# A five-layer perceiver block: the last stage's weights rounded during the sign MLP and kept in device memory

## The reference, cut to what matters

```python
# sign MLP: weights are +1 or -1 by a boolean (k0, k1, k2)
h = s0 * _conn_dense(k0, concatenate([x, -x])); h = relu(h) * 2
h = s1 * _conn_dense(k1, h);                    h = relu(h) * 2
h = s2 * _conn_dense(k2, h)                     # 1024 -> 2048 -> 2048 -> 512

def _act_fake_quant(x, clip_factor):
    scale = sigmoid(clip_factor) * max(abs(x)) / 127
    return clip(round(x / scale), -128, 127) * scale
def _weight_fake_quant(w):
    scale = max(abs(w), axis=1, keepdims=True) / 127
    return clip(round(w / scale), -128, 127) * scale
xq   = _act_fake_quant(x, clip_x)
gate = einsum('bsh,ih->bsi', xq, _weight_fake_quant(w_gate))     # w_gate, w_up: 1408 x 512
up   = einsum('bsh,ih->bsi', xq, _weight_fake_quant(w_up))
h    = _act_fake_quant(silu(gate) * up, clip_down)
out  = einsum('bsi,hi->bsh', h, _weight_fake_quant(w_down))      # w_down: 512 x 1408
```

## Time and profile before

| what | value |
|---|---|
| time, median of 3 runs | 1179.59 us (1178.83 to 1183.53) |
| profiled execution, its own time | 1179.79 us |
| its span in the profile | 1178.0 us |
| mean granted clock of TensorE | 0.974 of full speed |
| sign MLP: end of its second half's layer 0 / of its output layer | 489.2 / 627.4 us |
| last stage: first instruction / end | 1060.7 / 1178.0 us |

### The profile page before, as it was taken

One profiled execution on the slowest core, in us unless ns is written; L12 is line 12 of the kernel. 1 busy time (PEld: TensorE's weight loads), 2 busy tenths in 40 slices (PEclk: granted clock), 3 DMA queues, 4 the chain that ended last, 5 costly groups with the idle time before them and its releaser, 6 DMA issues. The chain is left out here.

```text
span 1178.0 us, 17300 instructions
## 1 busy us (share of the span) xinstructions
PE 1080.0 (92%) x6279; PEld 679.8 (58%) x6300; DVE 597.3 (51%) x1020; ACT 388.1 (33%) x1038; POOL 214.9 (18%) x205
## 2 busy tenths in 40 slices
PE   7899999999899999999999999776898989985976
PEld 4456568887444444444445655374796968663542
DVE  2344356786733222421113544277658484758857
ACT  1222245666310001201001322243324232337863
POOL 0111101333322310070000111043141221200004
PEclk9899999999999999999999999978999999996999
DMA  9966802001011100300034788340000000008001
GB/s 337 386 231 228 299 1 73 1 1 37 27 36 42 38 0 1 103 13 0 0 143 143 265 304 296 149 163 1 2 0 1 0 0 0 0 0 294 1 1 71
DMA packets 55127, 108.60 MB, mean 92 GB/s; under 512 B 4144, under 2 KB 4528, under 8 KB 55088
## 3 DMA queue, kind: packets, MB, share of 16 engines
q1 hardware_dynamic: 55088, 108.09, 25.9%
HBM read 105.98 MB, written 2.10 MB: 92 GB/s over the span
## 5 line engine op out<-in xcount | busy, mean ns | idle before, releaser
L1769 ACT ACTIVATE f_act<-bank,f_sgn 128x512 f32<-128x512 f32 x64 | 44.0, 687 | 267.8 <-PE bank L1724 262.3
L1724 PE MATMUL bank<-f_a_hi,f_w 128*128 128x512 f16 x512 | 115.7, 379 | 0.0
L1724 PE MATMUL bank<-f_a_lo,f_w 128*128 128x512 f16 x512 | 115.7, 379 | 0.0
L1798 DVE CAST f_b_hi<-f_act 128x512 f32 x32 | 27.1, 848 | 164.3 <-ACT f_act L1769 164.3
L1724 PEld LDWEIGHTS bank<-f_a_lo,f_w 128*128 x512 | 50.1, 98 | 60.4
L1724 PEld LDWEIGHTS bank<-f_a_hi,f_w 128*128 x512 | 50.1, 98 | 60.2
L1574 DVE TENSOR_TENSOR s_e<-s_pair,s_tables 128x512 f32<-128x512 f32 x64 | 41.4, 687 | 42.0 <-POOL s_kT L1634 24.8
L397 PE MATMUL bank<-x_cT,x_qT 128*64 128x512 f32 x256 | 60.0, 613 | 0.0
L422 PE MATMUL bank<-x_cN,x_eT 128*64 128x512 f32 x256 | 56.9, 596 | 0.0
L698 POOL TENSOR_TENSOR x_mv<-x_mv,eps 128x2 f32<-128x2 f32 x9 | 1.7, 193 | 292.8 <-DVE x_mv L568 292.8
L1456 ACT ACTIVATE s_e<-bank,s_nmax 128x64 f32<-128x64 f32 x128 | 38.0, 336 | 50.8 <-DVE s_nmax L1520 50.8
(11 more groups left out here) (337 smaller groups left out, 2305.3 us busy)
## 6 DMA issues: line engine op xcount, KB each, us to landing
x_cT<-in_ctx_cols_dram SPq DMA_DIRECT2D x32, 1024.0 KB, 8.2
x_cN<-in_ctx_rows_dram SPq DMA_DIRECT2D x32, 1024.0 KB, 9.7
f_upper_bits<-in_f_w_dram SPq DMA_DIRECT2D x20, 256.0 KB, 2.7
s_wv_raw<-in_s_wv_dram SPq DMA_DIRECT2D x3, 1024.0 KB, 10.3
f_raw<-in_f_wd_dram SPq DMA_DIRECT2D x1, 2816.0 KB, 17.6
x_qw<-in_x_qw_dram SPq DMA_DIRECT2D x8, 256.0 KB, 4.8
x_kw<-in_x_kw_dram SPq DMA_DIRECT2D x8, 256.0 KB, 5.6
x_vw<-in_x_vw_dram SPq DMA_DIRECT2D x2, 1024.0 KB, 9.6
```

The lines of the kernel that those rows point to most:

```text
L1724: mm = pe.matmul(h_bank[s][:, :], weights(2 * i + s, k), part[:, k, cols], start=(n == 0 and k == 0), stop=(n == 1 and k == k_chunks - 1))
L1769: act.activation(act32[s][:, :], h_bank[s][:, :], ACT.Relu, scale=sgn[:, layer % 2:layer % 2 + 1]).then_inc(h_read, 1)
L1798: dve.tensor_copy(hi[:, 2 * i + s, :], act32[s][:, :]).then_inc(hhi_ok, 1)
```

## The change

The last stage no longer scales, rounds and transposes weights. A new class `Rounding` keeps, through the whole kernel, the row maxima, steps and inverses of the three matrices, and reserves device memory for the three rounded bf16 matrices in the layout of the matmul (`[P, KC, I]`, `[P, KC, I]`, `[P, IC, D]`). The host passes, beside the raw matrices, their transposes (`f1_wgT`, `f1_wuT`, `f1_wdT`). Working buffers lie over the sign MLP's first-layer weights, booleans and first-layer inputs.

In `sign_mlp`:
- SyncE, once the booleans of layer 2 are converted, loads the 26 row chunks of the raw matrices (22 of [128, 512] in four slots, 4 of [128, 1408] in one), stores the inverses of the three matrices and the steps of down to device memory, and waits for that. After `h_done >= 3 * HC` it loads, for each of 27 parts of the transposed matrices (8 + 8 of [128, 704], 11 of [128, 512]), the part, and at the start of a matrix the broadcast row of its inverses; it stores the rounded parts. Two buffers alternate for parts in and for parts out. It ends with a wait for all stores, ahead of the next stage's loads.
- VectorE takes the row maxima, 22 of them between the output tiles of the first half and 4 before layer 1 of the second, and then makes steps and inverses.
- GpSimd takes each part through a product with the inverse row, an addition and a subtraction of 1.5 * 2^23, the last one to bf16, each behind a wait for the one before; at its end it waits for all stores.

In `quantized_ffn` SyncE loads the clip scalars, gate, up, the row of down steps and down. ScalarE's first wait is for the clip scalars and the row of steps. Tokens are transposed through four banks instead of two, and the products of chunk 0 wait for their half of the tokens alone.

```diff
+class Rounding:
...
+        half = I // 2
+        self.matrices = []
+        for rows, cols, kept in ((io["f1_wg"], io["f1_wgT"], self.gate), (io["f1_wu"], io["f1_wuT"], self.up)):
+            parts = [{"width": half, "span": I, "at": slice(h * half, (h + 1) * half), "src": cols[k * P:(k + 1) * P, h * half:(h + 1) * half],
+                      "dst": kept[:, k, h * half:(h + 1) * half]} for k in range(KC) for h in range(2)]
...
         @block.sync
         def _(sp):
...
+            sp.wait_ge(w2_ok, W2_RAW)
+            for n, (m, c) in enumerate(rows):
+                slot = n % RAW if m < 2 else 0
+                if n >= RAW:
+                    sp.wait_ge(wmax_ok, n - RAW + 1 if m < 2 else n)
+                sp.dma_start(maxima_raw[m][slot], matrices[m]["rows"][c]).then_inc(row_in[slot], 16)
+            sp.wait_ge(wstep_ok, 4)
+            for m in range(3):
+                sp.dma_start(rounding.inverse_out[m], w_inv[m], allow_slow_non_contiguous=True).then_inc(inv_out, 16)
+            sp.dma_start(rounding.step_out, w_step[2], allow_slow_non_contiguous=True).then_inc(inv_out, 16)
+            sp.wait_ge(inv_out, 16 * 4)
+            sp.wait_ge(h_done, 3 * HC)
+            for n, (m, a) in enumerate(parts):
+                part = matrices[m]["parts"][a]
+                if a == 0:
+                    if n:
+                        sp.wait_ge(scaled_ok, n)
+                    sp.dma_start(inv_row[:, 0:part["span"]], rounding.inverse_row[m].partition_broadcast(P)).then_inc(inv_in, 16)
+                if n >= 2:
+                    sp.wait_ge(rounded_ok, 2 * (n - 1))
+                sp.dma_start(raw_part[n % 2][:, 0:part["width"]], part["src"]).then_inc(part_in[n % 2], 16)
+                if n:
+                    last = matrices[parts[n - 1][0]]["parts"][parts[n - 1][1]]
+                    sp.wait_ge(rounded_ok, 2 * n)
+                    sp.dma_start(last["dst"], rounded_out[(n - 1) % 2][:, 0:last["width"]]).then_inc(part_out[(n - 1) % 2], 16)
...
+            sp.wait_ge(part_out[0], 16 * ((len(parts) + 1) // 2))
+            sp.wait_ge(part_out[1], 16 * (len(parts) // 2))
...
         @block.vector
...
+                    if half == 1 and layer == 1:
+                        row_maxima(range(2 * HALF_ROWS, len(rows)))
+                        dve.wait_ge(wmax_ok, len(rows))
+                        dve.tensor_scalar(rounding.all_step, rounding.all_max, 1.0 / QMAX, None, ALU.mult).then_inc(wstep_ok, 1)
...
+                    if half == 0:
+                        row_maxima(range(2 * HALF_ROWS * t // (HT // P), 2 * HALF_ROWS * (t + 1) // (HT // P)))
...
         @block.gpsimd
...
+            for n, (m, a) in enumerate(parts):
...
+                pool.wait_ge(inv_in, 16 * (m + 1))
+                pool.wait_ge(part_in[n % 2], 16 * (n // 2 + 1))
+                pool.tensor_tensor(raw_part[n % 2][:, 0:width], raw_part[n % 2][:, 0:width], inv_row[:, part["at"]], ALU.mult).then_inc(scaled_ok, 1)
+                pool.wait_ge(scaled_ok, n + 1)
+                pool.tensor_scalar(raw_part[n % 2][:, 0:width], raw_part[n % 2][:, 0:width], ROUND, None, ALU.add).then_inc(rounded_ok, 1)
+                pool.wait_ge(rounded_ok, 2 * n + 1)
+                if n >= 2:
+                    pool.wait_ge(part_out[n % 2], 16 * (n // 2))
+                pool.tensor_scalar(rounded_out[n % 2][:, 0:width], raw_part[n % 2][:, 0:width], ROUND, None, ALU.subtract).then_inc(rounded_ok, 1)
...
+def quantized_ffn(core, tag, weights, clips, out):
...
         @block.sync
         def _(sp):
             sp.dma_start(clip_in[:, :], clips.partition_broadcast(P)).then_inc(small_in, 16)
-            for g, cs in enumerate(groups):
-                at = slice(cs[0], cs[-1] + 1)
-                for m in range(2):
-                    sp.dma_start(raw[m][:, at, :], views[m][:, at, :]).then_inc(raw_in[m][g], 16)
-            sp.dma_start(raw[2][:, :, :], views[2]).then_inc(down_in, 16)
+            sp.dma_start(gT[:, :, :], weights.gate).then_inc(gate_in, 16)
+            sp.dma_start(uT[:, :, :], weights.up).then_inc(up_in, 16)
+            sp.dma_start(d_row[:, :], weights.step_row.partition_broadcast(P)).then_inc(small_in, 16)
+            sp.dma_start(dT[:, :, :], weights.down).then_inc(down_in, 16)
...
         @block.scalar
-            act.wait_ge(small_in, 16)
+            act.wait_ge(small_in, 32)
             act.activation(clip_s[:, :], clip_in[:, :], ACT.Sigmoid).then_inc(clip_ok, 1)
```

More of the change, by code:

```diff
@@ L740, in cross_attention, with __init__ @@
         return x_ok
+class Rounding:
+    def __init__(self, core, stack, io):
+        nc = core.nc
+        I = io["f1_wg"].shape[0]
+        IC = I // P
+        self.I, self.IC = I, IC
+        counts = (IC, IC, KC)
+        firsts = (0, IC, 2 * IC)
+        maxima, steps, inverses = (core.sbuf(stack, f"f1_w_{n}", [P, sum(counts)]) for n in ("max", "step", "inv"))
+        of = lambda t: [t[:, f:f + n] for f, n in zip(firsts, counts)]
+        self.w_max, self.w_step, self.w_inv = of(maxima), of(steps), of(inverses)
+        self.all_max, self.all_step = maxima[:, :], steps[:, :]
+        internal = lambda n, s, d=F32: nc.dram_tensor(f"f1_{n}", s, d, kind="Internal").ap()
+        inverse = [internal(f"inverse{m}", [P * n]) for m, n in enumerate(counts)]
+        step = internal("step", [P * KC])
+        self.inverse_row, self.step_row = inverse, step
+        by_partition = lambda v: v.rearrange("(c p) -> p c", p=P)
+        self.inverse_out, self.step_out = [by_partition(v) for v in inverse], by_partition(step)
+        self.gate, self.up = (internal(n, [P, KC, I], BF16) for n in ("gate_rounded", "up_rounded"))
+        self.down = internal("down_rounded", [P, IC, D], BF16)
+        half = I // 2
[3 more added lines that the diff above has]
+                      "dst": kept[:, k, h * half:(h + 1) * half]} for k in range(KC) for h in range(2)]
+            self.matrices.append({"rows": [rows[c * P:(c + 1) * P, :] for c in range(IC)], "parts": parts})
+        parts = [{"width": D, "span": D, "at": slice(0, D), "src": io["f1_wdT"][c * P:(c + 1) * P, :], "dst": self.down[:, c, :]} for c in range(IC)]
+        self.matrices.append({"rows": [io["f1_wd"][c * P:(c + 1) * P, :] for c in range(KC)], "parts": parts})
+        right = lambda st, n, s, d=F32: st.enter_context(nc.sbuf_tensor(f"f1_{n}", s, d, side="right"))
+        with ExitStack() as early:
+            right(early, "over_w0", [P, 2 * KC, D])
+            slots = [right(early, f"rows{n}", [P, D])[:, :] for n in range(KC)]
+        with ExitStack() as early:
+            right(early, "over_w0_again", [P, 2 * KC, D])
+            row = right(early, "long_row", [P, I])[:, :]
+        self.maxima_raw = [slots, slots, [row]]
+        with ExitStack() as early:
+            right(early, "over_w0_third", [P, 2 * KC, D])
+            self.raw_part = [right(early, f"part{n}", [P, half]) for n in range(2)]
+            first = right(early, "rounded0", [P, half], BF16)
+            right(early, "over_bits", [P, 4 * D - 2 * half - half // 2])
+            right(early, "over_sign_rows", [P, 4 * D + 160])
+            self.inv_row = right(early, "inv_row", [P, I])
+            self.rounded_out = [first, right(early, "rounded1", [P, half], BF16)]
@@ L1653, in sign_mlp @@
     RAW = KC
+    HALF_ROWS = rounding.IC
     with ExitStack() as st:
@@ L1688, in sign_mlp @@
         W2_RAW = HC * D // H
+        maxima_raw, raw_part, rounded_out, inv_row = rounding.maxima_raw, rounding.raw_part, rounding.rounded_out, rounding.inv_row
+        w_max, w_step, w_inv, matrices = rounding.w_max, rounding.w_step, rounding.w_inv, rounding.matrices
+        row_in = [sem(f"row_in{n}") for n in range(RAW)]
+        wmax_ok = sem("weight_max_ok")
+        wstep_ok = sem("weight_step_ok")
+        inv_out = sem("inverse_out")
+        inv_in = sem("inverse_in")
+        part_in = [sem(f"part_in{n}") for n in range(2)]
+        scaled_ok = sem("scaled_ok")
+        rounded_ok = sem("rounded_ok")
+        part_out = [sem(f"part_out{n}") for n in range(2)]
+        rows = [(m, c) for m in range(3) for c in range(len(matrices[m]["rows"]))]
+        parts = [(m, a) for m in range(3) for a in range(len(matrices[m]["parts"]))]
         @block.sync
@@ L1787, in split_last, with row_maxima @@
                                       ALU.subtract).then_inc(xlo_ok, 1)
+            def row_maxima(which):
+                for n in which:
+                    m, c = rows[n]
+                    slot = n % RAW if m < 2 else 0
+                    dve.wait_ge(row_in[slot], 16 * (1 + sum(1 for j in range(n) if (j % RAW if rows[j][0] < 2 else 0) == slot)))
+                    dve.tensor_reduce(w_max[m][:, c:c + 1], maxima_raw[m][slot], AX_X, ALU.max, apply_absolute_value=True).then_inc(wmax_ok, 1)
             for half in range(HALVES):
@@ L2222, in program @@
         rows = lambda w: w.rearrange("(c p) n -> p c n", p=P)
+        rounding = Rounding(core, stack, io)
```

(3 more changed lines are left out.)

180 lines of the change are left out of this document (38 added, 142 removed).

## The result

The changed kernel takes 1254.5 us (median of 4 runs, 1253.6 to 1255.5), the kernel before beside it 1180.7 us (4 runs). The ratio is 1.0623, with an interval of 1.0598 to 1.0648: slower by some 74 us. The forecast was 1204 us, slower by 24. The direction and the place are right, the size is three times the forecast.

What follows compares the result with a forecast made beforehand. TensorE is busy 92% of the span, but ScalarE holds back the last stage; GpSimd's rounding would delay the next stage. 1179.8 + 43.9 (late hand-over) + 0.5 (row maxima) - 20.6 (last stage) = 1203.6, forecast 1204 us, range 1175 to 1256.

Steps and rivals of the forecast that it cites:

- T: End of GpSimd's rounding of the 27 weight parts during the sign MLP, forecast at 641.5 us; break-even was 618.
- The work behind T: Next stage's weight loads, GpSimd's mixes, 1/std and normalization after the rounding: transposes forecast to start 42.0 us after T.
- step 3: GpSimd's rounding of 27 parts, three dependent instructions each, one-input passes at 1.3 ns a column: 107 us in sum.
- the changes of matrix: Waits in GpSimd's rounding where a new inverse row loads only after the last product: two, at 2 us each.
- overlap with VectorE: Lengthening of GpSimd's rounding instructions by VectorE's casts running beside them: 5 us.
- step 1: Store of the inverses to device memory as 3840 pieces of 4 bytes: 17 us, bounds 2.5 and 23.
- step 2: Load of the broadcast inverse row and the first part before GpSimd starts: 5.3 us, start at 534.5.
- TensorE's slow start: Extra time at the second cross attention after TensorE idles at the hand-over: 1.5 us.
- The passes are slow: Rival: GpSimd's one-input rounding passes cost 3.05 ns a column, T = 696 and 1258 us; chance 0.22.
- The hand-over nearly in time: Rival: passes at 0.93 ns and a 2.5 us inverse store, next stage 10 us late, 1171 us; chance 0.18.
- The store at 50 us: Rival: storing the inverses as single values costs say 200 ns each, 50 us, giving 1237 us; chance 0.06.
- It is 26 if the step row came with the clips: Last stage: its forecast gain of 20.6 us would be 26 with the down-step row loaded alongside the clip scalars.

Runs made afterwards that it cites:

- the last experiment: Changed kernel with step row loaded first, inverses transposed before their store, next stage's loads ahead, and parts rounded on VectorE instead of GpSimd: 1157.1 us, ratio 0.9816 to the kernel before.

## Why the prediction went wrong in size

**Where it was right.** The place and the mechanism: the sum was made on T, and every experiment that moved T or the work behind it moved the time with it. VectorE was forecast to be done with steps and inverses at 512.2 and was done at 511.7. The row maxima cost layer 1 0.2 us (first matmul at 489.41 instead of 489.24), where 0.5 were forecast; since the same matmul starts anywhere from 485.3 to 490.6 in the other traces, this shows only that the cost is small. The work behind T was forecast at 42.0 us and took 39.9 (729.17 - 689.25). The first product of the last stage was forecast 22.7 us into it and came 22.8 in. The whole last stage gained 18.1 us; 20.6 were forecast.

**The step that failed: step 3, the price of a one-input pass.** The prediction put the add and the subtract at 1.3 ns a column, between the uint8 conversion (0.93) and the f32 product with a scalar of each partition (3.05), "nearer to the first". They cost 2.9. The form with a constant gains almost nothing on a scalar of each partition; both f32 and bf16 outputs are slow. The pass with two operations (3.8 ns) has the very form of the uint8 conversion (0.93 ns), two constants and a bf16 output, so what the slow rows share is the f32 input. Whether it is the type alone, or also the wider tile of that row, was not tried. A wide part takes 5.8 us instead of 4.0 and a narrow one 4.4 instead of 3.0. The sum, by its terms: 16 x 5.8 + 11 x 4.4 + 1.1 for the changes of matrix = 142.3, against 142.5 in the trace; 107 were forecast. The 4 us for the changes of matrix and the 5 for overlap with VectorE hardly came (the first pass takes 2.31 us, the mean 2.01). So 35.5 of the 50 us that the forecast lacked are step 3. The price of the passes alone was further off than that: all passes together were put at 43.9 us and are 96.7, 52.8 more. Some 17 us of it are hidden by terms that were put too high: the gaps between dependent instructions (12.2 forecast, 4 measured), the changes of matrix, the overlap, and 0.9 of the product. That is luck. Taking both passes away gained 64.2 us, merging them 32.7.

The trace of before had a second f32 row, which the prediction overlooked. It speaks of two prices for a one-input pass, and of 3.05 as the only f32 row, but this one, subtract and multiply with two scalars of each partition, costs 2083 / 512 = 4.07 ns a column. From the view by form of the kernel before:

```profile
L1122 POOL TENSOR_SCALAR s_fn<-xres,s_fmv 128x512 f32<-128x512 f32 x6 | 12.5, 2083 | 0.3
```

With it, two f32 rows stood against one uint8 row, and the two rows with two operations each, 0.93 ns from uint8 and 4.07 from f32, already differed by a factor of four.

Of the pass, the Trainium skill (GPSIMD Engine Reference, section 4.1, Engine selection) says that GpSimd is roughly at line rate on one input. The trace of the changed kernel shows 2.9 ns a column for f32, over three times the 0.83 ns that the prediction had as an estimate from this rule, so here the measurement decides against the rule. Its advice to give elementwise work to VectorE agrees with the last experiment, 1.62 us a wide part against 5.8.

**The second term: step 1, the inverse store.** 17 us were forecast, 29.0 were measured, above the upper bound of 23. The bound took 240 pieces an engine at the mean time of a packet, 89 ns. From the trace after, (29.0 - 1.9) / 240 is 113 ns a piece, an estimate that leaves the time of the four issues in. The steps were ready 0.5 us sooner than forecast. With step 2 (6.1 instead of 5.3 us from the issue of the inverse row to GpSimd's first product), GpSimd starts 12.3 us later than forecast. Storing longer pieces took 25.2 of the 29.0 us away. Why a piece takes longer than a mean packet is not shown.

**Together.** T came 12.3 + 35.5 = 47.8 us later. The work behind it took 2.1 less. TensorE's slow start cost 3.8 where 1.5 were put down (the stage is 88.1 late at the transposes and 91.9 at its end), 2.3 more. The loss lies ahead of the next tile's transposes: they follow 16.3 us behind the first instead of 12.4, and in the last experiment, where TensorE does not wait, 12.4 again. In the last stage 2.5 were missing, chiefly in the chunks: 41.7 us for the 11 (1175.37 to 1217.1) against 39.6. The first chunk took 6.4 us, 2.9 more than the others, where 1.5 were allowed, and each of the others 3.52 instead of 3.46. The row maxima give back 0.5, which the 91.9 hold already. 47.8 - 2.1 + 2.3 + 2.5 - 0.5 = 50.0, and 73.8 - 23.8 = 50.0.

**The rivals.** "The passes are slow" was the right one: at 3.05 ns it had T = 696 and 1258 us, close to the 689 and 1254 measured. Part of that closeness is luck: its 27 parts and changes of matrix took 161 us, which leaves out the 5 us of overlap that the forecast counts, against 142.5 measured, and its start at 534.5 was 12.3 too early. The measured time lies inside the stated range, 1175 to 1256, only because this rival had stretched it. It was given 0.22 against 0.54 for the forecast, on the argument that a constant in place of an operand makes the instruction like the uint8 row. Two of the signs by which the prediction called itself wrong came: passes outside 0.9 to 1.7 ns, and a store over 25 us. The hand-over nearly in time (0.18) needed passes of 0.93 ns and a store of 2.5 us, and had neither. The store at 50 us (0.06) was too far. "It is 26 if the step row came with the clips" held in what the edit adds: 5.8 us against 5.4. The whole gain is 23.9 (93.4 instead of 117.3), short by about what the stage already lacked without the edit.

## What to carry to other kernels

Work that is moved "behind" another engine's stage is free only if the queue that it joins has nothing urgent behind it: here SyncE's queue held the next stage's weights and GpSimd's its mixes, and 40 us of them were pushed out together. Price an instruction by a row with the same input type before one of the same form, and where two rows are a factor of three apart, let both have their own forecast. If an idle engine's passes are too slow, look whether the busy one has gaps: VectorE was busy for 38 us with what kept GpSimd busy for 137.

## What the runs showed of the hardware

- GpSimd's one-input passes on f32 are slow whatever the second operand is: 2.9 ns a column with a constant, 3.05 with a scalar of each partition, 3.8 with two operations on constants in one instruction (2649 ns for 704), 4.07 with two on scalars of each partition (2083 ns for 512), and the output type does not matter (2012 ns to f32, 1983 to bf16). VectorE does the same two-operation pass for 704 columns in 0.53 us at the quickest (at 542.71), 0.75 ns a column, and in 0.67 in the mean.
- 3840 pieces of 4 bytes to device memory took 29.0 us, in the other runs that stored them so 24 to 28; the same values in pieces of 32 took 3.8, and 5.6 and 6.0 in the two runs in which the next stage's loads were issued just ahead. The packets under 512 B fell from 9328 to 5612, by about the 3720 pieces that were saved.
- VectorE and GpSimd hold each other up. In the kernel that rounds on VectorE, the same GpSimd instruction takes 1.56 us where VectorE is idle but for a cast at its end, and 2.53 while VectorE works on a part, and VectorE's product takes 1.97 us instead of 0.88. GpSimd's timeline and then VectorE's of this kernel:

```profile
531.62 1.56 POOL L718 TENSOR_SCALAR x_term<-x_kw,x_bq 128x512 f32<-128x512 f32 x1 [0.17 <-POOL x_k_mix L718]
...
534.75 2.53 POOL L718 TENSOR_SCALAR x_term<-x_kw,x_bq 128x512 f32<-128x512 f32 x1 [0.17 <-POOL x_k_mix L721]
...
540.60 1.27 POOL L721 TENSOR_TENSOR x_k_mix<-x_k_mix,x_term 128x512 f32<-128x512 f32 x1
```

```profile
540.64 1.97 DVE L1912 TENSOR_TENSOR f_part<-f_part,f_inv_row 128x704 f32<-128x704 f32 x1
...
543.15 0.88 DVE L1912 TENSOR_TENSOR f_part<-f_part,f_inv_row 128x704 f32<-128x704 f32 x1
```

  The product of 540.64 began just behind GpSimd's sum of 540.60 and ended 0.7 us after it, at 542.61. The Trainium skill (SBUF — State Buffer, section SBUF: two separate sides) states that the two share a pair of ports, which a VectorE instruction with two inputs in SBUF needs against a GpSimd instruction that reads SBUF, and that the one that comes second waits for the whole instruction of the other. The rows agree roughly: 1.23 us of waiting and 0.88 of work would be 2.1 us, against 1.97.
- After TensorE had stood idle, the granted clock was 0.50, its lower level of 1.2 GHz. In windows of the changed kernel (the clock is the third number from the end of each row): 0.50 from 729 to 735 and again from 1175 to 1180, and 1.00 from 1185 to 1190:

```profile
729.00:735.00 6.00, 5.83 (x22) 4.81 (x23) 4.35 (x9) 1.17 (x2) 0.00 (x0) 0.50 0.00 0
...
1175.00:1180.00 5.00, 4.63 (x11) 1.66 (x12) 2.35 (x4) 0.95 (x2) 0.00 (x0) 0.50 0.00 0
1185.00:1190.00 5.00, 5.00 (x24) 2.09 (x23) 3.15 (x6) 2.06 (x3) 0.00 (x0) 1.00 0.00 0
```
